# A two-batch prologue for a cross-attention kernel: keys projected ahead of queries, next values and turned rows inside the first score pass

## The reference, cut to what matters

```python
x = x + xattn(layernorm(x), ctx, ctx, ...)       # x, ctx: 8 batches x 256 rows x 256
x = x + ffn(layernorm(x), ...)                   # top-2 mixture of 8 experts, 256 -> 1024 -> 256

# xattn, 16 heads of 16
qh = (q @ W_q).reshape(B, S, 16, 16); kh = (k @ W_k)...; vh = (v @ W_v + b_v)...
scores = einsum('bihd,bjhd->bhij', qh, kh) / 4
keep = (j < i) | (i == 0) & (j == 0)
probs = softmax(where(keep, scores, -inf)); attn = einsum('bhij,bjhd->bihd', probs, vh)
return attn @ W_o + b_o
```

## Time and profile before

| what | value |
|---|---|
| time, median of 3 runs | 468.29 us (467.09 to 469.15) |
| the profiled execution's own time | 468.1 us |
| its span, first to last instruction | 466.4 us |
| PE busy in the span | 380.9 us (82%) |
| DVE, POOL, ACT busy | 296.0, 226.2, 188.1 us |
| steps 1 to 4 of the attention | 22.8 us each, from 71.43 us on |
| mean granted TensorE clock | 0.915 of full speed |

### The profile page before, as it was taken

How to read it: one execution, slowest core, us unless ns; L and a number is a source line. 1 busy time by engine, 2 the same in 40 slices (tenths; PEclk the granted TensorE clock), 3 DMA queues, 4 the chain that set the end, 5 groups by cost and what they waited for, 6 DMA issues and landing times. The chain is left out here.

```text
span 466.4 us, 8107 instructions
## 1 busy us (share of the span) xinstructions
PE 380.9 (82%) x3026; PEld 320.3 (69%) x3026; DVE 296.0 (63%) x616; ACT 188.1 (40%) x255; POOL 226.2 (48%) x311
## 2 busy tenths in 40 slices
PE   0576698999999999877532499999999999999992
PEld 0544467676777776655421279999999999999892
DVE  3545266767677666752339696677777777777841
ACT  3212344646565554545014053535353535353310
POOL 5672973838475755424003880444444444441432
PEclk9958799999999999999555589999999999999998
DMA  8620554516060609041210440454545454531232
GB/s 226 198 72 17 144 153 100 157 49 181 27 181 25 181 14 254 21 139 45 103 46 0 127 177 12 145 140 140 144 135 144 140 144 140 143 36 20 23 35 33
DMA packets 35735, 49.10 MB, mean 105 GB/s; under 512 B 4734, under 2 KB 31536, under 8 KB 34672
## 3 DMA queue, kind: packets, MB, share of 16 engines
q1 hardware_dynamic: 27744, 35.42, 25.2%
q0 software_dynamic: 6272, 8.57, 9.9%
q10 hardware_dynamic: 1680, 4.60, 3.1%
HBM read 27.57 MB, written 8.39 MB: 77 GB/s over the span
## 5 line engine op out<-in xcount | busy, mean ns | idle before, releaser
L1161 POOL DMA_INDIRECT out_dram<-Y,scatter_idx x32 | 51.8, 1619 | 102.8 <-DVE Y L1319 87.0
L1203 ACT ACTIVATE hr<-ps,b_sb 128x512 f32<-128x512 f32 x64 | 43.3, 687 | 101.6 <-PE ps L1378 64.7
L596 DVE TENSOR_REDUCE nm<-ps 128x2 f32<-128x512 f32 (+1 forms) x96 | 61.9, 684 | 16.0 <-PE ps L755 15.8
L1388 PE MATMUL ps<-w_hi,h_hi 128*128 128x256 f32 x224 | 64.0, 286 | 1.1 <-DVE h_lo L1294 1.1
L1388 PE MATMUL ps<-w_hi,h_lo 128*128 128x256 f32 x224 | 63.5, 283 | 0.0
L1388 PE MATMUL ps<-w_lo,h_hi 128*128 128x256 f32 x224 | 63.5, 283 | 0.0
L423 ACT ACTIVATE PT<-ps 128x1536 f32<-128x1536 f32 x32 | 46.4, 1451 | 25.3 <-PE ps L769 24.3
L1378 PE MATMUL ps<-XT_hi,w_hi 128*128 128x512 f32 x128 | 51.5, 402 | 1.5 <-DVE XT_lo L1281 1.5
L1378 PE MATMUL ps<-XT_hi,w_lo 128*128 128x512 f32 x128 | 51.3, 401 | 0.0
L1378 PE MATMUL ps<-XT_lo,w_hi 128*128 128x512 f32 x128 | 50.6, 395 | 0.0
L1292 DVE CAST h_hi<-hr 128x512 fp32r<-128x512 f32 x60 | 27.5, 458 | 35.1 <-ACT hr L1203 35.0
(11 more groups left out here) (190 smaller groups left out, 880.4 us busy)
## 6 DMA issues: line engine op xcount, KB each, us to landing
raw<-in_L_ffn_w_dram SPq DMA_DIRECT2D x12, 1024.0 KB, 7.7
raw<-in_L_ffn_w_dram ACTq DMA_DIRECT2D x4, 1024.0 KB, 5.5
Qs<-q_h SPq DMA_DIRECT2D x24, 128.0 KB, 2.5
Ks<-k_h SPq DMA_DIRECT2D x24, 128.0 KB, 2.5
c_sb<-in_ctx_dram SPq DMA_DIRECT2D x8, 256.0 KB, 2.8
Qs<-q_m SPq DMA_DIRECT2D x16, 128.0 KB, 2.5
Ks<-k_m SPq DMA_DIRECT2D x16, 128.0 KB, 2.6
xn_rows<-x2n SPq DMA_DIRECT2D x8, 256.0 KB, 2.5
```

Source lines behind the costliest of these rows:

```text
L596: dve.tensor_reduce(nm[:, tile, h:h + count], max_bank[u % 2].rearrange("p (h j) -> p h j", h=count), AX_X, ALU.max, negate=True).then_inc ...
L1161: pool.indirect_dma_start(out_rows[:, :], bass.IndirectOffsetOnAxis(ap=scatter_idx[q][:, j:j + 1], axis=0), Y[q][:, j, :], None, bounds_ch ...
L1203: act.activation(hr[c % 2][:, :], h_bank[c % 4], ACT.Relu, bias=b1_sb[q][:, c:c + 1]).then_inc(hr_ready, 1)
L1388: last = pe.matmul(y_bank[j // 2][:, (j % 2) * D:(j % 2 + 1) * D], a[c % 4][:, j * P:(j + 1) * P], w[q][:, c, :], start=(c == 0 and n == 0 ...
```

## The change

The steps now run from 0 on. What steps -2 and -1 did, and the projections of batch 1, is written out in a prologue ahead of them on each engine. The prologue has PSUM banks of its own for batches 0 and 1 (3, 4 and 5, which the second score pass doesn't use yet), and two buffers for the context and for the first layernorm's statistics. Keys go ahead of queries, on PE and in SP's copies. The three small tensors bv, bo and wg are loaded by SP and no longer by POOL; Wk, Wq, Wv are issued by ACT ahead of its first work; x is loaded in four pieces, the last (10 tiles) behind the copies of batch 1. DVE, not POOL, makes the context's remainder for the first two batches. In step 0 the projections of batch 2 stand further ahead. The diff shows, after the banks, SP's, POOL's and ACT's prologue, then DVE's step 0 and prologue, then PE's.

```diff
+    first_bank = [ps[:, 3, :], ps[:, 4, :], ps[:, 5, :]]
...
-        for s in range(-2, B + 1):
+        for s in range(B + 1):
...
+    def query_bank(s):
+        return first_bank[0] if s == -2 else bank[0] if s == -1 else bank[1]
+    def key_bank(s):
+        return first_bank[1] if s == -2 else bank[1] if s == -1 else bank[0]
+    def values_bank(s):
+        return first_bank[2] if s == -1 else first_bank[0] if s == 0 else bank[0]
     def first(s, n):
         return s < n
+    WEIGHT_ORDER = (1, 0, 2, 3)
...
+            load_context(0)
+            sp.dma_start(x_all[:, 2:4, :], x_tiles[:, 2:4, :]).then_inc(x1_loaded, 16)
+            load_context(1)
+            sp.dma_start(bv_bc[:, :], bv.rearrange("(a n) -> a n", a=1).broadcast_to([P, D])).then_inc(small_loaded, 16)
+            sp.dma_start(bo_bc[:, :], bo.rearrange("(a n) -> a n", a=1).broadcast_to([P, D])).then_inc(small_loaded, 16)
+            sp.dma_start(wg_sb[:, :, :], wg.rearrange("(k p) e -> p k e", p=P)).then_inc(small_loaded, 16)
+            sp.dma_start(x_all[:, 4:6, :], x_tiles[:, 4:6, :]).then_inc(x2_loaded, 16)
...
+                    for row in (stack_keys, stack_queries) if s < 0 else (stack_queries, stack_keys):
+                        row(s, to)
...
+            step(-2)
+            step(-1)
+            sp.dma_start(x_all[:, 6:, :], x_tiles[:, 6:, :]).then_inc(x_loaded, 16)
...
+            mask_constants()
+            fill_keys(0)
+            norm_powers(0)
+            buffer_constants(0)
+            norm_powers(1)
+            split_keys(-2)
+            fill_keys(1)
+            split_queries(-2)
+            split_keys(-1)
+            split_queries(-1)
+            norm_powers(2)
+            fill_keys(2)
+            zero_queries(2)
+            buffer_constants(1)
+            split_context(0)
+            add_bias(0)
+            add_bias(1)
+            routing_constants()
...
+            act.dma_start(w_raw[:, 1], Wk.rearrange("(k p) n -> p k n", p=P)).then_inc(wqkvo_loaded[1], 16)
+            act.dma_start(w_raw[:, 0], Wq.rearrange("(k p) n -> p k n", p=P)).then_inc(wqkvo_loaded[0], 16)
+            act.dma_start(w_raw[:, 2], Wv.rearrange("(k p) n -> p k n", p=P)).then_inc(wqkvo_loaded[2], 16)
...
+            round_weights(1)
+            round_context(-2)
             round_weights(0)
             norm_x(0)
-            round_weights(1)
+            round_weights(2)
+            round_keys(-2)
+            round_x(-2)
+            norm_x(1)
+            round_context(-1)
+            round_queries(-2)
+            round_x(-1)
+            round_weights(3)
+            round_keys(-1)
+            round_queries(-1)
+            round_context(0)
+            norm_x(2)
+            round_x(0)
+            copy_maxima(-1)
...
+                elif s == 0:
+                    maxima(s, 0)
+                    maxima(s, 1)
+                    split_queries(s)
+                    next_stats(s)
+                    maxima(s, 2)
+                    split_keys(s)
+                    maxima(s, 3)
+                    split_weights(3)
+                    dve.memset(x2n[:, :, :], 0.0).then_inc(x2n_stored, 16)
+                    maxima(s, 4)
+                    maxima(s, 5)
+                    split_maxima(s)
...
+            dve.wait_ge(x0_loaded, 16)
+            norm_stats(x_all[:, 0:2, :], st1[0], mv1[0], ln1_stats, 0)
+            split_weights(1)
+            split_context(-2)
+            split_weights(0)
+            next_stats(-2)
+            split_weights(2)
+            split_keys(-2)
+            split_x(-2)
+            split_context(-1)
+            split_queries(-2)
+            split_x(-1)
+            dve.memset(Qs[1][:, :, :].rearrange("p h t -> p (h t)").bitcast(F32), 0.0).then_inc(q_zeroed[1], 1)
+            add_value_bias(-1)
+            split_keys(-1)
+            maxima(-1, 0)
+            split_queries(-1)
+            maxima(-1, 1)
+            next_stats(-1)
+            maxima(-1, 2)
+            maxima(-1, 3)
+            maxima(-1, 4)
+            maxima(-1, 5)
+            split_maxima(-1)
+            add_value_bias(0)
+            split_x(0)
...
+                if s == 0:
+                    pe.wait_ge(q_rest_ready, 1)
+                project(values_bank(s), 2, cT_hi, cT_lo, v_done)
             def outputs(s):
                 pe.wait_ge(aT_lo_ready, s)
+                if s == 1:
+                    pe.wait_ge(w_lo_ready, 4)
                 project(bank[1], 3, aT_hi, aT_lo, op_done)
             def router(s):
@@ -906,15 +976,24 @@
                 last.then_inc(rt_done, 1)
             def step(s):
-                if s == -1:
-                    project_values(s)
-                    turn_x(s)
+                if s == 0:
                     a_scores(s, 0)
-                    for pair in range(1, UNITS // 2):
-                        a_scores(s, pair)
+                    queries(s)
+                    b_scores(s, 0)
+                    a_scores(s, 1)
+                    keys(s)
+                    b_scores(s, 1)
+                    a_scores(s, 2)
+                    values(s, 0)
+                    a_scores(s, 3)
+                    b_scores(s, 2)
+                    values(s, 1)
+                    a_scores(s, 4)
+                    b_scores(s, 3)
+                    a_scores(s, 5)
+                    values(s, 2)
                     turn_maxima(s)
-                    queries(s)
-                    keys(s)
+                    values(s, 3)
...
+            keys(-2)
+            turn_x(-2)
+            project_values(-1)
+            queries(-2)
+            turn_x(-1)
+            keys(-1)
+            queries(-1)
+            a_scores(-1, 0)
+            project_values(0)
+            a_scores(-1, 1)
+            a_scores(-1, 2)
+            a_scores(-1, 3)
+            a_scores(-1, 4)
+            turn_x(0)
+            a_scores(-1, 5)
+            turn_maxima(-1)
```

More of the change, by code:

```diff
@@ L76, in attention @@
     half = sb("half", [P, 2], F32)
-    c_sb = sb("c_sb", [P, 2, S], F32)
+    c_sb = [sb(f"c_sb{q}", [P, 2, S], F32) for q in range(2)]
     xn = sb("xn", [P, 2, D], F32)
[L79 to L82, removed]
+    st1 = [sb(f"st1_{q}", [P, 2, 6], F32) for q in range(2)]
+    mv1 = [sb(f"mv1_{q}", [P, 2, 2], F32) for q in range(2)]
+    ve1 = [sb(f"ve1_{q}", [P, 2, 2], F32) for q in range(2)]
+    rs1 = [sb(f"rs1_{q}", [P, 2, 2], F32) for q in range(2)]
     st2 = sb("st2", [P, 2, 6], F32)
@@ L111, in attention @@
     idx8 = sb("idx8", [P, 2, 8], U32)
-    x0_loaded, x_loaded = sem("x0_loaded"), sem("x_loaded")
-    ctx_loaded = sem("ctx_loaded")
+    x0_loaded, x1_loaded, x2_loaded, x_loaded = sem("x0_loaded"), sem("x1_loaded"), sem("x2_loaded"), sem("x_loaded")
+    ctx_loaded = [sem(f"ctx_loaded{q}") for q in range(2)]
     wqkvo_loaded = [sem(f"w{n}_loaded") for n in "qkvo"]
@@ L205, in step, with stack_keys @@
+            def stack_keys(s, to):
+                sp.wait_ge(k_filled[to], 1)
+                sp.wait_ge(k_h_ready, s + 3)
+                stack(Ks[to], K_PARTS, "h", k_part["h"], k_stacked)
+                sp.wait_ge(k_m_ready, s + 3)
+                stack(Ks[to], K_PARTS, "m", k_part["m"], k_stacked)
+                sp.wait_ge(k_l_ready, s + 3)
+                stack(Ks[to], K_PARTS, "l", k_part["l"], k_stacked)
             def step(s):
                 to = (s + 2) % BUFS
-                if proj_part(s) and s + 3 < B:
+                if s + 4 < B:
@@ L360, in step @@
                     mask(s, 1)
-                if s == -1:
-                    norm_powers(2)
-                if proj_part(s) and s > -2:
+                if proj_part(s):
                     split_queries(s)
@@ L504, in step @@
                 else:
-                    if proj_part(s):
+                    if proj_part(s) and s > 0:
                         round_context(s)
@@ L519, in step @@
                         normalise_x2(s)
-                    if proj_part(s):
+                    if proj_part(s) and s > 0:
                         round_keys(s)
-                    if first(s, -1):
-                        round_weights(3)
                     if out_part(s):
@@ L711, in step @@
                         maxima(s, 1)
-                    if first(s, -1):
-                        split_weights(2)
                     if proj_part(s):
                         split_queries(s)
-                    if proj_part(s) and not first(s, -1) and not (s + 3 >= B):
+                    if s + 3 < B:
                         next_stats(s)
```

172 lines of the change are left out of this document (64 added, 108 removed).

## The result

| what | before | after |
|---|---|---|
| median of 4 executions each | 468.71 us (467.09 to 469.15) | 454.17 us (450.4 to 458.8) |
| profiled execution | 468.1 us | 450.4 us |
| its span, mean granted clock | 466.4 us, 0.915 | 448.3 us, 0.933 |

The ratio after to before is 0.9665 [0.9627, 0.9702] (it leaves out the 458.8, which counts as a slow execution; the table's median has it). The prediction was 453.3 us, 449.4 to 459.5. A second measurement of the same kernel gave 451.4 us against 469.91, ratio 0.9638 [0.959, 0.9686]. So the kernel is faster by 14.5 to 18.5 us.

A forecast was written before the change was run, and what follows sets the result against it. PE bounds the steady steps, so only the 71.43 us ahead of step 1 were to shrink, to 56.3: -6.9, +2.5, -4.6 and -6.0, together -15.0 us. That gave 453.3 us, range 449.4 to 459.5.

The forecast's parts named there:

- The bound: PE sets the steady step (20.82 of 22.78 us), so only the 71.43 us ahead of step 1 change; 395.0 us stay.
- (a): Start of batch 0's first score pass: keys and their copies go first, so it starts at 21.9 instead of 28.84, -6.9 us.
- keys 1 us before 7.6: Start of batch 0's keys if DVE's context remainder need not wait for POOL's fill; pass perhaps 0.7 us earlier, not in sum.
- (b): First score pass to split maxima: grows from 11.0 to 13.5 us with next values, queries' rest and statistics inside, +2.5 us.
- (c): From the maxima to the second score pass: 3.6 us with hand-overs instead of 8.2, second pass at 39.0, -4.6 us.
- (d): Step 0: batch 1's 4.43 us stall goes and POOL's queue sets the end; 17.3 instead of 23.3 us, -6.0 us.
- 13 to 17 of the forecast: Gain in us over the kernel before that counts as the forecast itself, given a chance of 0.52.
- rival 3: Prologue at full clock with earlier weights: (a) 8, (b) +1, step 1 at 52.5, time 449.4 us; chance 0.08.
- rival 2: First pass doesn't start earlier because copies land when they did; (a) near 0, gain 8, time 460.3 us; chance 0.07.
- rival 1: Low clock and hand-overs ahead of step 1 take part: step 1 at 58.5 to 62, gain 9 to 13, 457.3 us; chance 0.28.
- Rivals 2 and 4: 2: first pass no earlier, 460.3 us, 0.07. 4: slower, POOL's queue delays the second pass's mask, about 470 us, 0.03.
- DVE's reductions and POOL's fills lock each other out: A sub-case of the slower rival, ahead of the second pass's mask: it could cost 3 to 5 us, not 15.

## Why the prediction was right, and where not

*The bound.* Right: only what lies ahead of step 1 moved, and the steps behind it kept their 395 us.

*(a) -6.9, measured -7.85.* The chain was right link by link. The keys' projection starts at 7.51 (7.6 predicted), their rounding ends at 11.07 (11.0), SP's key copies end at 15.02 (14.9), the last copy is issued at 18.44 and that issue ends at 19.05 (19.35). What I counted wrong is the landing: 2.5 us is from the start of an issue, and I added it to the end. Here it is 20.99 - 18.44 = 2.55. That is 0.6 of the 0.9 us between 21.9 and 20.99; the other 0.3 is the earlier last issue.

A DVE remainder beside a POOL fill takes its plain time. The timelines of DVE and POOL, and ACT's for what the keys waited for:

```profile
14.04 0.69 DVE L605 TENSOR_TENSOR cT_lo<-c_sb,cT_hi 128x512 fp32r<-128x512 f32 x1 [1.39 <-ACT cT_hi L431]
```

```profile
13.66 1.81 POOL L278 MEMSET Ks<- 128x2048 f32 x1
```

```profile
6.10 0.63 ACT L431 ACTIVATE cT_hi<-c_sb 128x512 fp32r<-128x512 f32 x1 [0.93 <-DMA c_sb<-in_ctx_dram]
```

The remainder lies wholly inside the fill and takes 0.69 us, as against the 1.73 beside a bias. With that agrees the Trainium skill (SBUF — State Buffer, "SBUF: two separate sides"), by which a DVE instruction with two SBUF inputs is locked out only by a GpSimd instruction that reads SBUF. What it would have brought, keys 1 us before 7.6, did not come: ACT's rounding of the context waited for its landing until 6.10. Nor did batch 0's remainder, at 6.76, have a fill beside it; POOL's fill of the keys ended at 5.43.

*(b) +2.5, measured +0.1.* This term of the sum was mis-sized. My 13.5 us for the pass has the next values at half clock and DVE idle for 1.4 us of them. The clock was full, and DVE, which sets the pace of the pass, hardly waited for them:

```profile
21.54 1.29 DVE L635 TENSOR_REDUCE nm<-ps 128x2 f32<-128x512 f32 x2 [1.72 <-PE ps L822]
22.74 0.68 DVE L613 TENSOR_TENSOR q_rest<-ps,q_h 128x512 f32<-128x512 f32 x1
23.70 1.29 DVE L635 TENSOR_REDUCE nm<-ps 128x4 f32<-128x512 f32 x2 [0.28 <-PE ps L822]
```

The values run on PE from 21.59 to 23.05, under the first reductions and the rest of batch 1's queries; DVE idles 0.28 us behind them. That full clock explains only half of the miss, since by my own working it takes 1.2 us off and leaves 12.3. The rest is that I added to the 11.0 us of before and left its waits in. There DVE works 8.94 us and idles 2.09, and a remainder of batch 1's rows (0.69 us at 29.71) is part of the work; in after it works 9.71 and idles 1.40, although the queries' rest and the statistics came in. The cost of the values at half clock was about right: with the queries' copies first DVE waits 1.81 us for the second pair, and the pass takes 12.2 to 12.7 at 0.86 or 0.87 with the values in it, 11.1 without them.

*(c) -4.6, measured -3.7.* The order was right; hand-overs took 4.54 us, not 3.6. The reason is the first trip of the small copy, whose issue by ACT is longer:

```profile
32.94 1.25 ACTq L504 DMA_DIRECT2D Qs<-nmT  x1
...
54.48 0.62 ACTq L504 DMA_DIRECT2D Qs<-nmT  x1
```

From its start to its use it is 3.70 us for the first and 2.55 for a later one. Before, too, the first one took 1.24 us, which I had not looked up.

*(d) -6.0, measured -6.6.* Step 0 took 16.74 us for the 17.3 predicted. POOL's queue was what ended it, as predicted: from the second mask on its chain is 9.9 us (9.8), and taking 1.8 out of it shortened step 0. Its chain ahead of the first mask is 12.2 us (12.5) and begins at 26.16, not 29.0, so it holds nothing up. The half clock at its end, here from 50.11, made the last values and the next projections slow:

```profile
50.11:56.94 6.83, 5.02 (x32) 4.03 (x32) 0.59 (x1) 2.14 (x5) 1.61 (x5) 0.52 0.45 94
```

*The sum* is -18.05 for -15.1 in this execution, which is outside the 13 to 17 of the forecast and near rival 3, "full clock and earlier weights". The medians of 454.17 and 451.4 lie on both sides of the 453.3, since other executions of the same kernel were 2 to 8 us longer; they had the lower mean clocks, but whether the clock is the whole cause is not shown. The upper end of the range, 459.5, is called the end of rival 2, whose time is 460.3; it is near the upper end of rival 1 (a gain of 9, 459.3). An estimate from the mean clock: (1 - 0.933) x 2 x 448.3 = 60 us of a 450.4 us execution were at half clock. In the 455.88 one (span 453.8, clock 0.911) it was 81 us, and before (0.915 of 466.4) 79. So the gain of the profiled execution holds for six of twelve, and rival 1, a low clock that takes part of it, fits the others. That the error of (b) and that of the spread cancelled in the median is luck.

*Rivals 2 and 4* fell: the first pass does start earlier, and the first mask waits for the exponential, not for POOL's constants. Nor did DVE's reductions and POOL's fills lock each other out: the six reductions from 25.92, in part beside fills (from 27.83 on), took 3.95 us, 0.66 each, as against 0.65 for the two of 1.29 at 21.54.

## What to carry to other kernels

Where two operands are copied through one queue, copy first the one that can be ready first: the queue is the chain, and the order that let it stand idle cost 4.2 us here and a slower pass behind it. Work out every span of a launch phase twice, once at each level of the clock, and take out of the old span the waits that the new order fills. Compare an execution's mean granted clock before you explain a few microseconds between two versions. Don't let a large load be under way while small copies are on the path: 1.25 MB moved to the front of the same queue cost 6 us of 450.

## What was not expected of the hardware

- A transfer's issue on SP took 5.29 us while a 1.25 MB load issued just before it was under way, for 0.37 us without; the twelve 128 KB copies behind it then took 5.1 to 8.1 us to land instead of 2.4 to 3.4.
- ACT's first issue of the small copy took 1.25 us, the next 0.62, in before (1.24) as in after.
- Without the values in it the first pass took 11.1 us at a clock of 0.86, as long as at 1.00 with them; with them and 0.86 or 0.87 it took 12.2 to 12.7.
- Executions of one kernel fell in a group at 450.26 to 450.40 us with clock 0.932 or 0.933 (six of twelve) and others up to 458.8 with 0.911. Where the extra half-clock time lies in those was not seen.
